# Three attention layers: own product and message summed in one PSUM bank per four columns, end mask moved into the states and the bias, shorter softmax

## The reference

```
for l in range(3):                        # attention layers, HEADS = 2, HEAD_DIM = 128
    q, k, v = x @ Wq + bq, x @ Wk + bk, x @ Wv + bv
    e = edge_weight @ We
    alpha = (q[dst] * (k[src] + e)).sum(-1) / sqrt(128)
    a = softmax of alpha over the edges of one dst
    msg = segment_sum((v[src] + e) * a, dst).mean over heads
    h = elu(msg + x @ Wskip + bskip)
    x = layer_norm(x + h) * ln_g + ln_b
```

## Time and profile before

| | |
|---|---|
| median of 3 runs | 6719.53 us |
| span of the profiled execution | 6709.9 us, mean granted TensorE clock 0.847 |
| VectorE busy | 5671.2 us (85%) |
| TensorE busy (products) | 4854.9 us (72%) |
| ScalarE busy | 4713.5 us (70%) |
| GpSimd busy | 4189.3 us (62%) |
| attention layers, from the load of their weights | 1570, 2504 and 3426 us to about 4538 us |
| angle layer | about 5480 us to the end |

### The profile page before, as it was taken

How to read it: one execution, slowest core, us unless ns; L and a number is a source line. 1 busy time by engine, 2 the same in 40 slices (tenths; PEclk the granted TensorE clock), 3 DMA queues, 4 the chain that set the end, 5 groups by cost and what they waited for, 6 DMA issues and landing times. The chain is left out here.

```text
span 6709.9 us, 115105 instructions
## 1 busy us (share of the span) xinstructions
PE 4854.9 (72%) x27083; PEld 3619.1 (54%) x27083; DVE 5671.2 (85%) x28706; ACT 4713.5 (70%) x13694; POOL 4189.3 (62%) x4100
## 2 busy tenths in 40 slices
PE   4133233333999978999969988867997769888881
PEld 1022222223777756778846666645564547666661
DVE  9857777774999978999969999985776869999996
ACT  0017777874999977999958999973554647878784
POOL 7767777755666626555446666617773445777774
PEclk8555555556999989999979999988998989999995
DMA  3359996554777744555535666645665964444441
GB/s 102 97 115 162 168 169 129 127 118 124 214 219 215 220 146 154 190 190 188 172 121 167 183 184 180 178 128 172 206 209 197 299 213 140 152 145 150 142 152 42
DMA packets 645498, 1104.01 MB, mean 165 GB/s; under 512 B 268429, under 2 KB 403416, under 8 KB 644690
## 3 DMA queue, kind: packets, MB, share of 16 engines
q1 hardware_dynamic: 507730, 816.19, 39.8%
q0 software_dynamic: 137088, 280.47, 17.9%
HBM read 578.27 MB, written 544.97 MB: 167 GB/s over the span
## 5 line engine op out<-in xcount | busy, mean ns | idle before, releaser
L1884 POOL DMA_INDIRECT xs<-tab,rec x1176 | 1235.0, 1050 | 652.2 <-issue 287.1
L2005 ACT ACTIVATE z<-p_a 128x512 f32<-128x512 f32 x1176 | 696.5, 592 | 251.6 <-PE p_a L1790 242.4
L1999 ACT ACTIVATE st<-xs,cb 128x128 f32<-128x128 f32 x2352 | 808.5, 396 | 0.7 <-DVE cg L1582 0.7
L1941 PE MATMUL p_y<-w_all,xt 128*128 128x258 f32 x2352 | 725.7, 390 | 32.4 <-DVE cA L2077 31.8
L1938 PE MATMUL p_a<-w_all,xt 128*128 128x256 f32 x2352 | 732.6, 394 | 19.3 <-ACT xt L1990 15.9
L2112 DVE SCALAR_TENSOR_TENSOR st<-st,cg 128x128 f32<-128x128 f32 x2352 | 709.9, 341 | 6.1 <-ACT st L1999 5.3
L2077 DVE CUSTOM_DVE_ANT_0 junk<-p_y,xs 128x129 f32<-128x129 f32 x2352 | 578.0, 281 | 16.5 <-PE p_y L1941 14.6
L1016 PE MATMUL p_m<-b_rows,ones_bf 3*128 3x512 bf16 x224 | 100.3, 448 | 674.6 <-ACT z L1059 674.5
L1794 PE MATMUL p_m<-w_all,z 128*128 128x128 f32 x2352 | 579.8, 329 | 0.0
L2692 POOL DMA_INDIRECT xs<-res,rec x392 | 423.2, 1079 | 192.2 <-issue 89.0
L1790 PE MATMUL p_a<-ident,st 128*128 128x128 f32 x2352 | 460.7, 278 | 95.8 <-DVE st L2112 95.6
(11 more groups left out here) (763 smaller groups left out, 16528.5 us busy)
## 6 DMA issues: line engine op xcount, KB each, us to landing
states<-st SPq DMA_DIRECT2D x168, 910.0 KB
own<-tab SPq DMA_DIRECT2D x168, 448.0 KB
tab<-o SPq DMA_DIRECT2D x168, 448.0 KB
runs<-run SPq DMA_DIRECT2D x112, 448.0 KB
tab<-out SPq DMA_DIRECT2D x112, 448.0 KB
x<-tab SPq DMA_DIRECT2D x112, 448.0 KB, 5.0
xd<-tab SPq DMA_DIRECT2D x168, 192.0 KB, 3.8
angles<-st SPq DMA_DIRECT2D x56, 532.0 KB, 2.8
```

The lines of the kernel that those rows point to most:

```text
L1884: pool.indirect_dma_start(xs[:, i, j, 0:D], None, table, bass.IndirectOffsetOnAxis(ap=rec[:, i, SRC, j : j + 1], axis=0)).then_inc(got_in[ ...
L1941: ins = pe.matmul(p_y[two(c, i)][:, 0 : H * X1], xt[:, two(c, i), 0:D], k.w_qk[:], start=True, stop=True)
L1999: ins = act.activation(state_of(r, j)[:, h, :], xs[:, c.slot(UB), j, 0:D], ACT.Copy, scale=co.b[:, c.slot(2), h, j : j + 1])
L2005: act.activation(z[:, c.slot(RING), j, :], p_a[two(c, j)][:], ACT.Copy).then_inc(st_copied, 1)
```

## The change

1. TensorE's own product into `p_a` keeps only the residual half. x @ Wskip is made in `value`, straight into the message's bank. Four columns, then three, share a bank (`GROUPS`), and `p_m`'s two banks are the two groups. `xt` has four buffers instead of two, since the own half is read again two columns later.
2. The bias is one product a group: a block-diagonal `b_block` against the rows `end_rows`, which hold END of each column (three times, for the three bf16 parts of the bias), so that it falls on end edges only. `setup` transposes END and writes these rows to memory; SP loads two small blocks of them a chunk.
3. `add_own` is gone. The message's state is 2^-70 times smaller at inner edges: the reciprocal is multiplied by END + 2^-70 and the carried factor by 2^70, so that the unmasked message adds nothing there that f32 would show. `merge_parts` multiplies by 2^70.
4. The exponential is taken from PSUM in two pieces (after columns 3 and 6), `positive` too, into a new ring `y`. `z` has 3 x 128 columns and a ring of 2 instead of 4 x 128 and 4.
5. The softmax adds the mask before the exponential instead of multiplying after it, and writes into the tiles that the scan reads: 13 small VectorE instructions a chunk instead of 14, and 12 in the angle layer. The dead `Coef.level` is dropped.

The core of the diff:

```diff
+                act.wait_ge(end_turned, 1)
+                for i in range(END_BLOCKS):
+                    n = min(END_COLS, COLS - i * END_COLS)
+                    ins = act.activation(end_t[0:n, i, :], part_ps[0:n, i * P : (i + 1) * P], ACT.Copy)
+                ins.then_inc(end_copied, 1)
+                act.wait_ge(end_copied, 1)
+                for i in range(END_BLOCKS):
+                    a, z = i * END_COLS, min((i + 1) * END_COLS, COLS)
+                    for s in range(3):
+                        act.dma_start(k.end_rows[a:z, s, :], end_t[0 : z - a, i, :]).then_inc(end_out, 16)
...
+                pe.wait_ge(ended, 1)
+                for i in range(END_BLOCKS):
+                    a, z = i * END_COLS, min((i + 1) * END_COLS, COLS)
+                    ins = pe.transpose(part_ps[0 : z - a, i * P : (i + 1) * P], end[:, a:z], k.ident[:])
+                ins.then_inc(end_turned, 1)
...
+        self.fa = sb("cfa", [P, 2, H, J + 1])
...
+        self.ex = self.fa[:, :, :, 1:].rearrange("p s h j -> p (s h) j")
...
         elif n == 2:
-            dve.tensor_tensor(self.ex[:, 0], m[:, :, 0:J], m[:, :, 1:], ALU.subtract)
-            self.at = order.put(dve.tensor_tensor(self.ex[:, 1], self.A[:, i, :, 1:], m[:, :, 1:], ALU.subtract))
+            self.at = order.put(dve.tensor_tensor(f[:, :, 1:], m[:, :, 0:J], self.neg[:, :, 1:], ALU.add))
+            dve.tensor_tensor(a[:, :, 1:], self.A[:, i, :, 1:], m[:, :, 1:], ALU.subtract).then_inc(exp_in, 1)
         elif n == 3:
-            dve.tensor_scalar(self.ex[:, 0], self.ex[:, 0], 0.0, None, ALU.min).then_inc(exp_in, 1)
+            dve.tensor_tensor(f[:, :, 1:], f[:, :, 1:], m[:, :, 1:], ALU.subtract).then_inc(exp_in, 1)
         elif n == 4:
-            dve.tensor_tensor(self.f[:, :, 1:], self.ex[:, 0], same, ALU.mult)
-            self.at = order.put(dve.tensor_copy(self.a[:, :, 1:], self.ex[:, 1]))
+            self.at = order.put(dve.tensor_tensor_scan(self.flat(z[:]), self.flat(f), self.flat(a), 0.0, ALU.mult, ALU.add))
         elif n == 5:
-            self.at = order.put(dve.tensor_tensor_scan(self.flat(z[:]), self.flat(self.f[:]), self.flat(self.a[:]), 0.0, ALU.mult, ALU.add))
+            dve.reciprocal(self.rz[:], z[:, :, 1:])
+            self.at = order.put(dve.scalar_tensor_tensor(self.h[:], f[:, :, 1:], 1.0 / self.small, z[:, :, 0:J], ALU.mult, ALU.mult))
         elif n == 6:
-            dve.reciprocal(self.rz[:], z[:, :, 1:])
-            self.at = order.put(dve.tensor_tensor(self.h[:], self.f[:, :, 1:], z[:, :, 0:J], ALU.mult))
+            if self.small != 1.0:
+                self.at = order.put(dve.scalar_tensor_tensor(self.rz[:], self.wide(end), self.small, self.rz[:], ALU.add, ALU.mult))
         elif n == 7:
-            dve.tensor_tensor(self.b[:, i], self.a[:, :, 1:], self.rz[:], ALU.mult)
+            dve.tensor_tensor(self.b[:, i], a[:, :, 1:], self.rz[:], ALU.mult)
...
-            step(dve.tensor_tensor(part(w, g), part(w, g), each(inv, g, P), ALU.mult))
+            step(dve.scalar_tensor_tensor(part(w, g), part(w, g), 1.0 / co.small, each(inv, g, P), ALU.mult, ALU.mult))
...
-        xt = tile("xt", [P, 2, 2 * D])
+        xt = tile("xt", [P, 4, 2 * D])
...
-        z, e, o = tile("z", [P, RING, J, 4 * D]), tile("e", [P, 2, J, D]), tile("o", [P, RING, J, D])
+        z, e, o = tile("z", [P, 2, J, 3 * D]), tile("e", [P, 2, J, D]), tile("o", [P, RING, J, D])
+        y = tile("y", [P, RING, J, D])
+        end_rows = tile("end_rows", [3 * GROUPS[0][1], RING, NG, P], BF16)
+        b_block = tile("b_block", [3 * GROUPS[0][1], GROUPS[0][1] * D], BF16)
...
-        w_loads = [(k.w_all[:], k.conv_w[l]), (k.b_msg[:], k.conv_b[l])]
+        w_loads = [(k.w_all[:], k.conv_w[l])]
+        b_loads = [(b_block[3 * i : 3 * i + 3, i * D : (i + 1) * D], k.conv_b[l]) for i in range(GROUPS[0][1])]
...
+                        wait(sp, m_made, c.count(NG, NG - RING * NG), passed)
+                        for g, (a, z_) in enumerate(GROUPS):
+                            sp.dma_start(end_rows[0 : 3 * (z_ - a), c.slot(RING), g, :],
+                                         k.end_rows[c.n * J + a : c.n * J + z_].rearrange("c s p -> (c s) p")).then_inc(end_rows_in[c.slot(RING)], 16)
...
-                        ins = pe.matmul(p_a[two(own_c, own_i)][:, 2 * D : 4 * D], xt[:, two(c, i), D : 2 * D], k.w_own[:], start=True, stop=True)
+                        ins = pe.matmul(p_a[two(own_c, own_i)][:, 2 * D : 3 * D], xt[:, four(c, i), D : 2 * D], k.w_own[:, D : 2 * D],
+                                        start=True, stop=True)
...
-                    wait(pe, z_done, c.count(J, j - 1))
-                    pe.matmul(p_m[two(c, j)][:, 0:D], k.ones_bf[:], k.b_msg[:], start=True, stop=False)
+                    g = group_of(j)
+                    a, z_ = GROUPS[g]
+                    if j == a:
+                        if g == 0:
+                            pe.wait_ge(end_rows_in[c.slot(RING)], (c.use(RING) + 1) * 16 * NG)
+                        wait(pe, z_done, c.count(NG, g + 1 - NG))
+                        pe.matmul(p_m[g][:, 0 : (z_ - a) * D], end_rows[0 : 3 * (z_ - a), c.slot(RING), g, :],
+                                  b_block[0 : 3 * (z_ - a), 0 : (z_ - a) * D], start=True, stop=False)
+                    out_ = p_m[g][:, (j - a) * D : (j - a + 1) * D]
+                    pe.matmul(out_, xt[:, (four(c, j) + SCORE * J + 1) % 4, D : 2 * D], k.w_own[:, 0:D], start=False, stop=False)
                     pe.wait_ge(st_copied, c.count(J, j + 1))
-                    value_product(pe, two(c, j), at_of(c, j)).then_inc(m_made, 1)
+                    ins = value_product(pe, out_, at_of(c, j), j == z_ - 1)
+                    if j == z_ - 1:
+                        ins.then_inc(m_made, 1)
 
...
-                    act.activation(z[:, c.slot(RING), j, :], p_a[two(c, j)][:], ACT.Copy).then_inc(st_copied, 1)
+                    if j in (GROUPS[0][0], GROUPS[1][0]):
+                        wait(act, z_done, c.count(NG, group_of(j) + 1 - 2 * NG))
+                    act.activation(z[:, c.slot(2), j, :], p_a[two(c, j)][:, 0 : 3 * D], ACT.Copy).then_inc(st_copied, 1)
+
+                def exponential(c, g):
+                    a, z_ = GROUPS[g]
+                    act.wait_ge(m_made, c.count(NG, g + 1))
+                    if g == 0:
+                        wait(act, resid, c.count(1, -1))
+                    act.activation(flat(e[:, c.slot(2), a:z_, :]), p_m[g][:, 0 : (z_ - a) * D], ACT.Exp).then_inc(e_out, 1)
 
...
-                        if j == 4 and c1.there:
-                            act.wait_ge(z_done, c1.count(J, J))
-                            wait(act, resid, c1.count(1, -1))
-                            act.activation(e[:, c1.slot(2)], part(c1, 2), ACT.Exp).then_inc(e_out, 1)
+                        if j == 6 and c0.there:
+                            exponential(c0, 0)
+                        if j == 2 and c1.there:
+                            exponential(c1, 1)
...
-                def add_own(c, j):
-                    v = part(c, 2)[:, j]
-                    dve.wait_ge(m_made, c.count(J, j + 1))
-                    dve.scalar_tensor_tensor(v, p_m[two(c, j)][:, 0:D], field(c, END)[:, j : j + 1], v, ALU.mult, ALU.add).then_inc(z_done, 1)
-
-                def positive(c):
-                    dve.wait_ge(z_done, c.count(J, J))
-                    at["positive"] = order.put(dve.scalar_tensor_tensor(part(c, 3), part(c, 2), 0.0, part(c, 3), ALU.max, ALU.add))
+                def positive(c, g):
+                    a, z_ = GROUPS[g]
+                    dve.wait_ge(e_out, c.count(NG, g + 1))
+                    if g == 0:
+                        wait(dve, norm.applied, c.count(1, 1 - RING))
+                    dve.scalar_tensor_tensor(y[:, c.slot(RING), a:z_, :], p_m[g][:, 0 : (z_ - a) * D].rearrange("p (j d) -> p j d", d=D), 0.0,
+                                             z[:, c.slot(2), a:z_, 2 * D : 3 * D], ALU.max, ALU.add).then_inc(z_done, 1)
 
                 def negative(c):
-                    order.land(at["positive"])
-                    dve.wait_ge(e_out, c.count(1, 1))
-                    dve.scalar_tensor_tensor(part(c, 2), e[:, c.slot(2)], 1.0, part(c, 3), ALU.min, ALU.add).then_inc(resid, 1)
+                    v = y[:, c.slot(RING)]
+                    dve.wait_ge(z_done, c.count(NG, NG))
+                    dve.scalar_tensor_tensor(v, e[:, c.slot(2)], 1.0, v, ALU.min, ALU.add).then_inc(resid, 1)
...
-                        cz, i = column(k, t, u, 0, j - 2)
-                        if cz.there:
-                            add_own(cz, i)
+                            level(co.THEN[j], mid)
...
-                        if j == 2 and c1.there:
-                            positive(c1)
+                        if j in (0, 4) and c1.there:
+                            positive(c1, group_of(j))
```

More of the change, by code:

```diff
@@ L30 @@
 FAR = float(1 << 20)
+SMALL = 2.0 ** -70
 LOW = -1.0e30
@@ L88 @@
```

(38 more changed lines are left out.)

88 lines of the change are left out of this document (33 added, 55 removed).

## The result

The changed kernel takes 6504.56 us, the median of 4 runs (6492.13 to 6522.17); the kernel before took 6718.67 beside it (4 runs, 6716.89 to 6723.35). The ratio is 0.9686, 95% interval 0.9669 to 0.9703 (that of the two medians is 0.9681): 214 us gained where 235 were forecast. The total is near the forecast, but the parts are not.

| stage | before | after | difference | forecast |
|---|---|---|---|---|
| setup, graph convolution | 1570.2 | 1578.3 | +8 | +2 |
| first attention layer | 934.3 | 850.0 | -84 | -65 |
| second | 921.1 | 836.4 | -85 | -76 |
| last | 1112.6 | 1099.1 | -14 | -88 |
| mean aggregation, batch norm | 938.5 | 940.2 | +2 | 0 |

The account below looks back on a forecast made before the run. VectorE was taken to bound all layers, TensorE right behind in the first two. Gains of 67, 78, 90 and 8 us, less 8 for setup and layer starts, gave 235: 6719.5 - 235 = 6484 us, range 6420 to 6590.

Parts of the forecast that it names:

- The two group products with their losses: TensorE's bias products of 512 and 384 columns, with losses at the bf16 step: 0.51 + 0.46 = 0.97 us a chunk.
- The second weight load: TensorE's new 128-column product costs nothing net if its weight load is hidden; otherwise 0.8 us a chunk more, 14.2.
- The choice between semaphore and bf16: TensorE's 0.09 and 0.11 us losses around the bias product were assigned to the f32/bf16 step, not to semaphore waits.
- The allowances: First layer allowed 13.8 us a chunk for GpSimd's gathers; second 13.6, with 0.2 above the larger engine for coupling.
- The rival of the gathers: GpSimd's gathers bound the first layer at 14.4 us a chunk and more, others as forecast: 6517 us, chance 0.12.
- that of TensorE's losses: TensorE keeps its losses, needs 14.2 to 14.6 us a chunk and bounds the first two layers: 6562 us, chance 0.15.
- that of no coupling: All engines give what their rows say: first two layers 13.3 us a chunk, last 16.4; total 6445 us, chance 0.1.
- One of TensorE's bounds: If none of the losses around TensorE's f32 products returns: 7 x 0.20 = 1.4 us a chunk more, 14.6.
- VectorE's saving: Masked add gone -1.8 us, second piece of the positive part +0.14, shorter softmax -0.08: net -1.74 us a chunk.
- Waits that are added: New waits of ScalarE's exponentials, VectorE's pieces and TensorE's bank reuse: all held free, bounds 0 and 0.5 us a chunk.
- a sign only for the first two layers: A clock under 1.00 in the first two attention layers was listed as showing the forecast wrong.
- The bound of 12: Angle layer's softmax loses a copy and a multiply: 8 us taken as gain, bounds 0 and 12.

Follow-up runs that it names:

- the same order: VectorE's last layer reordered (negative to column 3, second norm's statistics to 1, sums to 2): in the changed kernel 6409.65 us, in the kernel before 6697.94 us.
- filler: Changed kernel plus 16 idle identity transposes a chunk on TensorE in the last attention layer, where it waits for VectorE's second state: 6460.23 us.

## Why the prediction was right in sum and wrong in one part

**The total: near, in part by luck.** By the table, the first two layers and the angle layer brought 37 us more than forecast, and the last layer, setup and mean aggregation 82 less. That leaves 45 us too little, 189 instead of 235; that the medians have 214 is because the profiled execution before was shorter than its other runs and the one after the longest of four. The mechanism held for the first two layers and failed for the last.

**First and second layer: right.** TensorE's column was forecast at 1.75 us and is 1.77. The two group products with their losses were forecast at 0.97 a chunk: 0.10 + 0.32 + 0.10 and 0.10 + 0.26 + 0.10 make 0.98. Without them the chunk is 0.42 shorter and VectorE the bound, so they cost only the part above VectorE. The second weight load is hidden (0.22 for the pair, 0.23 for L1962). The choice between semaphore and bf16, made from the earlier trace rows, is confirmed. Measured pace 13.6 (720 adds in 700 us) and 13.5 against 13.8 and 13.6, so the gains were 84 and 85 instead of 65 and 76. 1.4 and 1.5 us times 56 are 78 and 84; where the remaining 6 us of the first are was not looked at. The allowances (for the gathers in the first, for coupling in the second) were 0.2 and 0.1 too large. The rival of the gathers and that of TensorE's losses fell, and that of no coupling held only for VectorE's 13.1 without the bias. One of TensorE's bounds was added up wrongly, without effect: 7 x 0.20 = 1.4 more counts the losses in the two group columns again, and 5 x 0.20 would have done.

**VectorE's saving: right.** With the same order in both kernels the last layer goes from 17.9 to 16.2 us a chunk, -1.7; forecast -1.74. The 512-element piece from PSUM takes 0.60 us to the next start (3526.63 to 3527.23), less than the 0.65 of the slope from the earlier trace rows. By an estimate from the Trainium skill's fixed costs (VectorE: DVE Perf Modes, TRN2 errata) an instruction should take 0.065 us more with a PSUM source than with an SBUF source. The trace doesn't show that: in full queues L2119, from PSUM, takes 0.26 to 0.27 to the next start, and L2137, all in SBUF, 0.265.

**The last layer: wrong, 14 us instead of 88.** The step that failed is "Waits that are added", which held the added waits free, with 0.5 us a chunk as their bound, and the old ones were not asked about; 17.9 - 16.6 = 1.3 was measured. VectorE's sum of work fell as forecast, but the layer no longer follows that sum. In the kernel before, VectorE's own 18.2 us a chunk covered TensorE's waits for its states (0.94 to 1.73 us once a chunk for the state of column 1, in 3550 to 4400 us). With 16.2 us of work it no longer covers them: the old order takes 16.9 us a chunk even where the clock stays up, and more where it falls. The two costs: 1099.1 - 1046.9 = 52 us for the clock (filler), and the other 49 for the waits, which only the order removed; the filler has some work of its own in it, so this division is rough.

Shown is that the same three edits of the order are worth 16 to 18 us in the kernel before and 101 in the changed one. Which part of the change made the difference is argued. Two things point the same way. The first piece of `positive`, looked at only as a wait for the exponential, is also 0.60 us of work, and it came into the column of VectorE that in this layer alone already held 3.34 us of long pieces; from the state of column 0 to that of column 1 it is 5.15 us now (3522.24 to 3527.39), 4.84 before (3911.59 to 3916.43). And TensorE's column went from 2.10 to 1.77 us, so that it has less work in store. The first alone is not enough: with `negative` moved, column 0 holds 2.94 us of long pieces, less than the 3.34 of the kernel before, and the layer is still 31 us above the one with the full order (1029.4 and 998.3). No run moved the first piece alone.

**The clock.** The prediction named a lower clock as a sign only for the first two layers, where it stayed at 1.00. The earlier trace rows had it at 0.97 in the last layer, the sign of standstills at hand, and no term was made of it; it is 0.91 now.

**Angle: 8 forecast, 17 measured.** Six executions with the new softmax have 1210.8 to 1221.2 us there, mean 1215.7, two with the old 1233.2 and 1228.0: 15. The new softmax alone, in the slower session, gave 18. From start to next start, the two instructions that are gone took 0.24 us a chunk; the rewritten clamp takes 0.03 more, and a small copy (L1611, L1588 before) 0.06 more. With some hundredths elsewhere that is 0.17 us, 9 us in all. The steady stretch

```profile
L2833 DVE TENSOR_TENSOR prod<-q,p_q 128x128 f32<-128x128 f32 x354 | 97.4, 275 | 45.0 <-ACT z L2778 44.5
```

has 950/(354/7) = 18.8 us a chunk. The 19.3 of the earlier trace rows was a slower stretch of its layer: from the first to the last of all 392 such instructions it is 19.1 before and 18.8 after (1067.1 and 1050.6 us), 16.5 us in all. The bound of 12 was too low, and 6 us are unexplained.

**Setup.** The end of the first stage was 8 us later in this execution, but at 1567.9 to 1577.8 in the five others with the same setup, and at 1570.2 and 1572.3 with the old: the scatter is as large as the difference, and 2 us can't be told from nothing.

## What to carry to other kernels

If an engine's work shrinks, waits that this work used to cover come to light: before counting on the new sum, look at the waits of the other engines that cost nothing so far. A piece of work that moves has two costs: its length in the engine's sum, and its length in the queue position where others wait behind it; look for the longest time between two things that the engine hands over, and compare it with how much work the receiver has in store, above all when the same change makes the receiver faster. Where a layer has steps that others don't have, work out the column that receives the moved piece in that layer too. If an engine is busy 99% before and the forecast leaves TensorE with more slack, ask what the granted clock will be, and put a step at another column before adding anything.

## What was not expected of the hardware

TensorE stood still for 0.77 us and, a column later, for 1.57, in nearly every chunk of the last layer. In some stretches the clock fell to half behind it (0.42 us a pair instead of 0.22; 19.0 us a chunk, mean clock 0.85), in others it stayed at 1.00 (17.0 us a chunk), with the same standstills. Sixteen useless transposes a chunk made the kernel 44 us faster. A 3-row bf16 product among f32 products costs 0.36 us with 0.16 of its own, and about the same 0.20 is lost around a 12-row one of 512 columns.
